# Layer 0's gated sums of rows, on four column groups instead of one

## The reference

```python
route_probs = jax.nn.softmax(xr @ wr.T, axis=-1)        # 8 routes
routes_k, indices_k = jax.lax.top_k(route_probs, 2)
gates = routes_k / jnp.sum(routes_k, axis=-1, keepdims=True)
h = jax.nn.silu(xr @ w1.T)
h = jax.nn.silu(h @ w3.T)
h = h @ w2.T
out = jnp.zeros_like(xr)
for k in range(2):
    out = out.at[indices_k[:, k]].add(gates[:, k:k + 1] * h)
```

## Time and profile before

| what | us |
|---|---|
| median of 3 runs (2851.77 to 2856.73) | 2856.41 |
| the profiled execution's own time | 2845.37 |
| its span in the profile | 2843.6 |
| TensorE busy | 2638.7 (93%) |
| VectorE busy | 1396.8 (49%) |
| ScalarE busy | 837.1 (29%) |
| layer 0 | about 0 to 1100 |
| layer 1 up to its experts | about 1100 to 1878 |

### The profile page before, as it was taken

One profiled execution on the slowest core, in us unless ns is written; L12 is line 12 of the kernel. 1 busy time (PEld: TensorE's weight loads), 2 busy tenths in 40 slices (PEclk: granted clock), 3 DMA queues, 4 the chain that ended last, 5 costly groups with the idle time before them and its releaser, 6 DMA issues. The chain is left out here.

```text
span 2843.6 us, 33688 instructions
## 1 busy us (share of the span) xinstructions
PE 2638.7 (93%) x10961; PEld 1346.8 (47%) x11021; DVE 1396.8 (49%) x2556; ACT 837.1 (29%) x1892; POOL 524.4 (18%) x563
## 2 busy tenths in 40 slices
PE   8999999999999766899999999759999999999998
PEld 4544554554455342334344334144465556655543
DVE  4546554573657263567777777507322222222255
ACT  2324332432343131145555555620011111111101
POOL 2111101110211001323233232000011111111053
PEclk9999999999999878899999999969999999999999
DMA  6120222132102103435545545240123333342155
GB/s 196 59 75 30 67 68 89 60 87 76 59 30 75 44 1 135 75 74 116 107 101 112 108 104 109 67 180 0 43 94 126 127 128 129 105 150 96 53 145 158
DMA packets 108460, 260.19 MB, mean 91 GB/s; under 512 B 19538, under 2 KB 53330, under 8 KB 96690
## 3 DMA queue, kind: packets, MB, share of 16 engines
q1 hardware_dynamic: 95634, 220.00, 26.2%
q0 software_dynamic: 11440, 37.50, 4.5%
q10 hardware_dynamic: 1264, 1.10, 0.1%
HBM read 203.27 MB, written 54.89 MB: 91 GB/s over the span
## 5 line engine op out<-in xcount | busy, mean ns | idle before, releaser
L2424 PE MATMUL d_bank<-d_w,d_xcol 128*128 x1264 | 402.5, 461 | 0.0
L1969 DVE TENSOR_REDUCE c_mx<-c_pair 128x2 f32<-128x1024 f32 x256 | 303.7, 1217 | 109.3 <-PE c_pair L1830 108.4
L1680 ACT ACTIVATE c_probs<-c_exp 128x512 f32<-128x512 f32 x512 | 277.9, 597 | 217.2 <-PE c_exp L1844 163.5
L2424 PEld LDWEIGHTS d_bank<-d_w,d_xcol 128*128 128x128 f32 x1264 | 229.0, 191 | 101.6 <-issue 2.0
L757 PE MATMUL a_bank<-a_xT,a_ring 128*128 128x512 f32 x608 | 272.5, 599 | 0.0
L508 POOL TENSOR_TENSOR a_ry<-a_rt 128x512 f32<-128x512 f32 x80 | 130.5, 1631 | 756.7 <-DVE a_rt L1009 756.7
L757 PE MATMUL a_bank<-a_wo,a_ot 128*128 128x512 f32 x512 | 222.4, 592 | 0.0
L2431 PE MATMUL d_bank<-d_w,d_hid 128*128 x480 | 219.1, 592 | 0.7 <-DVE d_hid L2662 0.7
L757 PEld LDWEIGHTS a_bank<-a_xT,a_ring 128*128 128x128 f32 x608 | 114.5, 192 | 132.3 <-issue 129.5
L2349 PE MATMUL d_bank<-d_xT,d_ws 128*128 128x512 f32 (+1 forms) x384 | 168.9, 600 | 0.7 <-ACT d_yrow L2326 0.7
L1844 PE MATMUL c_exp<-c_qs,c_ks 128*128 128x512 bf16 x453 | 146.7, 382 | 22.1 <-ACT c_probs L1680 7.9
(11 more groups left out here) (307 smaller groups left out, 3726.7 us busy)
## 6 DMA issues: line engine op xcount, KB each, us to landing
d_w<-in_w SPq DMA_DIRECT2D x16, 1408.0 KB, 6.7
scratch_results<-d_yrow SPq DMA_DIRECT2D x80, 256.0 KB
a_ring<-in_wq SPq DMA_DIRECT2D x16, 1024.0 KB, 4.8
a_wo<-in_wo SPq DMA_DIRECT2D x16, 1024.0 KB, 4.9
c_ks<-scratch_kpark SPq DMA_DIRECT2D x96, 128.0 KB, 4.7
c_qs<-scratch_qpark SPq DMA_DIRECT2D x96, 128.0 KB, 4.4
d_w<-in_w SPq DMA_DIRECT2D x16, 768.0 KB, 8.5
a_ring<-in_w SPq DMA_DIRECT2D x8, 1024.0 KB, 8.0
```

What stands on the lines that cost most here:

```text
L1680: act.activation(probs[:, (LC * CH * n + k) % RING, :], bank[:, :], ACT.Exp, scale=float(CD) ** -0.5).then_inc(exped.sem, 1)
L1969: dve.tensor_reduce(mx[:, n % 2, at0:at0 + 2], bank[:, :].rearrange("p (i n) -> p i n", i=2), AX.X, ALU.max).then_inc(maxed.sem, 1)
L2424: ins = pe.matmul(bank[:, 0:FI], xcol[:, v, k, :], w13[:, bass.ds(at, 1), which, k, :].rearrange("p a n -> p (a n)"), start=(k == 0), stop ...
```

## The change

The four matmuls of `first_rows` no longer add up in the same 8 partitions. `gate` becomes 32 columns wide for each sequence (columns 8 to 31 are zero and stay so; one GpSimd memset more, so `consts` counts ten). The matmul of sequence `b` writes the 32 partitions from `32 * b` on, each with start and stop. `fsum` becomes [128, 512] and so holds four parts, and the addition, the store, the scratch tensor and the load in layer 1 have that size. The four parts are summed where `fs` was turned: the transposes become fp32 matmuls with the constant `over` [128, 128], which has a one in rows 0 to 7, 32 to 39, 64 to 71 and 96 to 103, in the column of the route. `over` is loaded with one DMA more (64 KB). GpSimd's memset of `fs` goes, and with it SyncE's wait.

```diff
-        gate = sb("gate", [P, GB, E0])
-        fsum = sb("fsum", [E0, D])
+        gate = sb("gate", [P, GB, HD])
+        fsum = sb("fsum", [P, D])
...
-                    sp.wait_ge(consts.sem, 9)
+                    sp.wait_ge(consts.sem, 10)
...
+            pool.memset(gate[:], 0.0).then_inc(consts.sem, 1)
...
                     for b in range(GB):
-                        ins = pe.matmul(bank[0:E0, :], gate[:, b, :], h2[:, b, :], start=(b == 0), stop=(b == GB - 1))
+                        ins = pe.matmul(bank[HD * b:HD * b + HD, :], gate[:, b, :], h2[:, b, :], start=True, stop=True)
...
-                        ins = dve.tensor_tensor(gate[:, b, :], eq[:, 0, :], eq[:, 1, :], ALU.add)
+                        ins = dve.tensor_tensor(gate[:, b, 0:E0], eq[:, 0, :], eq[:, 1, :], ALU.add)
...
-                    dve.tensor_tensor(fsum[:, :], bank[0:E0, :], fsum[:, :], ALU.add).then_inc(f_added.sem, 1)
+                    dve.tensor_tensor(fsum[:, :], bank[:, :], fsum[:, :], ALU.add).then_inc(f_added.sem, 1)
...
+        over = probs[:, KC + 2, 0:P]
...
-            sp.wait_ge(consts.sem, NC)
-            sp.dma_start(probs[0:E0, KC, :], t["fsum"]).then_inc(fix_in.sem, 16)
+            sp.dma_start(fs, t["fsum"]).then_inc(fix_in.sem, 16)
+            sp.dma_start(over, t["over"]).then_inc(fix_in.sem, 16)
...
-            pool.memset(fs, 0.0).then_inc(consts.sem, 1)
...
-                        fix_in.wait(pe, 0, 3)
+                        fix_in.wait(pe, 0, 4)
                         bank = steps.start(pe, 0, ("ft",))
                         for c in range(KC):
-                            ins = pe.transpose(bank[:, c * P:(c + 1) * P], fs[:, c * P:(c + 1) * P], ident[:, :])
+                            ins = pe.matmul(bank[:, c * P:(c + 1) * P], fs[:, c * P:(c + 1) * P], over,
+                                            start=True, stop=True)
```

More of the change, by code:

```diff
@@ L537, in _ @@
             act.preload_act_table_set("natural_log_exp_and_others")
-            act.wait_ge(consts.sem, 9)
+            act.wait_ge(consts.sem, 10)
             for a, m in stages():
@@ L747, in _ @@
             pe.wait_ge(weights.sem, 16 * NW)
-            pe.wait_ge(consts.sem, 9)
+            pe.wait_ge(consts.sem, 10)
             for a, m in stages():
@@ L988, in _ @@
             dve.wait_ge(weights.sem, 16 * NW)
-            dve.wait_ge(consts.sem, 9)
+            dve.wait_ge(consts.sem, 10)
             for a, m in stages():
@@ L1375, in build_layer1 @@
         fs, ft = probs[:, KC, :], probs[:, KC + 1, :].rearrange("p (c n) -> p c n", c=KC)
+        over = probs[:, KC + 2, 0:P]
         rows = sb("rows", [E0, D])
         fstats, fmom, frstd = sb("fstats", [E0, 6]), sb("fmom", [E0, 2]), sb("frstd", [E0, 1])
-        NW, NL, NC, NS = 5, 4, 5, 2
+        NW, NL, NC, NS = 5, 4, 4, 2
         ident_in, weights, late = (signal(n, 0, 16) for n in ("ident_in", "weights", "late"))
@@ L2738, in build_program @@
     t = dict(t)
-    scratch = (("x3", [GROUPS, P, GB, D], F32), ("pre", [GROUPS, E0, D], F32), ("fsum", [E0, D], F32),
+    scratch = (("x3", [GROUPS, P, GB, D], F32), ("pre", [GROUPS, E0, D], F32), ("fsum", [P, D], F32),
                ("x5", [GROUPS, P, GB, D], F32), ("kpark", [2, P, 3, D], BF16), ("qpark", [2, P, 3, D], BF16),
@@ L2796, in constants @@
     t["ident16"] = high_halves(t["ident"])
+    t["over"] = np.zeros((P, P), f)
+    t["over"][HD * np.arange(GB)[:, None] + np.arange(E0), np.arange(E0)] = 1
     sel = np.zeros((MP, HX, P), f)
```

## The result

| | before | changed |
|---|---|---|
| median of 7 runs, us | 2856.41 (2851.77 to 2857.17) | 2845.06 (2840.74 to 2846.60) |
| ratio, with its 95% interval | | 0.9957 (0.9946 to 0.9969) |
| the profiled execution: time, span, us | 2845.37, 2843.6 | 2842.32, 2840.5 |

The change is faster by 11.3 us (difference of the medians; 0.4%), where 6.7 us were forecast; the time lies in the stated range of 2842 to 2855.5 us. Two later measurements of the same two kernels gave ratios of 0.9977 (0.9960 to 0.9995) and 0.9967 (0.9956 to 0.9979). The two profiled executions differ by 3.1 us only. So the questions are whether the steps of the forecast happened, and why executions of one kernel lie so far apart.

A forecast was written before the change was run, and what follows sets the result against it. Layer 0 was taken as bound by TensorE, busy 252.1 of 262.0 us in a stage. Terms -7.59 + 0.61 + 0.30 = -6.68 us, carried over to the median of 2856.41, gave 2849.7 us; range 2842 to 2855.5.

The forecast's parts named there:

- The product: Line 922's four matmuls, between stages of layer 0: 1.00 us to the successor instead of 3.53, saving 2.53 each.
- What follows it: Behind the product at three hand-overs between stages: everything moves 2.53 us earlier, waits keep their size, wider addition free; 7.59 saved.
- The third hand-over: Third passage between layer 0's stages, without keys, only VectorE's chain: 2.53 us saved, the 4.93 wait before the turning kept.
- The last product: Line 922's product in layer 0's last stage: saves 0, as VectorE's addition stands behind its late normalisation.
- The end store: Store of fsum at layer 0's end, 240 KB more behind the 1 MB store at 401 GB/s: +0.61 us.
- The turning: Turning of fs in layer 1, transposes replaced by fp32 products: 0.63 us becomes 0.93, so +0.30.
- The clock rival: Granted clock falls after hand-overs, 1.26 us each: two more give 2852.2 (chance 0.15), the present one vanishing 2848.4 (0.08).
- the prediction's own signs of being wrong: Layer 0's end moves by less than 5 us, or layer 1 or the experts change by more than 2.
- the forecast's own 2847 to 2852: Range for the whole program's time in us from the sum of the terms' bounds, without the slow store.
- a held stage: Rival: a transfer, such as the keys' weights, or another engine holds the next stage; two hand-overs lost, 2854.8 us, chance 0.08.

The follow-up runs named there:

- r4_vadd: Kernel before with the grouped product alone: fsum stays 8 by 512, VectorE adds the four parts one after another; 2847.18 against 2856.83 us, ratio 0.9972.
- r5_lastwide: Changed kernel with only the last stage's product undone, its four matmuls adding up over 128 columns again; ran once, 2850.14 us.
- r2_after: Changed kernel without an edit, measured again against the kernel before on the same chip; 2849.17 against 2856.83 us, ratio 0.9977.
- r1_before: Kernel before without an edit, run again for a second profile; ratio 0.9998 (0.9980 to 1.0016).
- r7_keys: Changed kernel with the fourth key tile ahead of turn_x(0) instead of behind it; 2838.57 against 2851.89 us, ratio 0.9952.

## Why the prediction was right, and where it was off

**The product, -2.53 us at a hand-over: right.** 257.4 to 254.9 in two stages, in two and three executions of the kernel before and the changed one. Layer 1's four-group products gave the price, 1.00, to the hundredth.

**What follows it: right.** The wait before the turning kept its size at both kinds of hand-over. That VectorE's wider addition costs nothing held within 0.01 us (0.69 against 0.68). r4_vadd shows how near VectorE's chain is.

**The third hand-over**: 2.49 us less from product to turning. The whole fourth stage is 128.1, 130.1 us before and 126.8, 128.2, 126.8 changed, 1.8 less in the mean; 2.5 is shown for its head only.

**The last product, 0: right**, by r5_lastwide.

**The end store, +0.61: 0.48 measured**, by the same two rows in seven profiles with the large store (8.74 to 8.76) and three with the small one and one addition (8.26 to 8.28). The price is the transfer: from its first packet to its last the two stores take 2.83 us before and 3.34 after, and from there to layer 1 it is 0.85 and 0.83. Whether the 240 KB more or their being in packets of 2 KB set the 0.51 is not shown; the forecast had the bytes at 401 GB/s.

**The turning, +0.30: 0.50 measured.** I compared lengths (0.63 with 0.93); the distances of starts are 0.56 and 1.06. The distance of starts is what a product takes from its successor, and this step did not keep to it.

**The clock rival.** It named the right mechanism and the right size (1.26 us then for the keys alone, 1.71 for a whole fall), but tied it to the hand-over. Falls come anywhere in layer 0. Their number differs by up to three in a stage, and the kernel before can be 11 us apart from itself in two profiles. That spread also trips one of the prediction's own signs of being wrong, a change of more than 2 us behind layer 0. From layer 1's start to the end the first profiles took 1743.3 and 1746.9 us, but the kernel before took 1748.1 in its second, so that sign could not tell anything.

**The size of the whole.** The steps sum to 2.53 + 2.53 + 2.49 - 0.48 - 0.50 = 6.6 us. Measured were 11.3, 7.7 and 9.5 us as differences of medians. That the first time lies in the stated range is in part luck: 2845.06 us is outside the forecast's own 2847 to 2852 (and its terms' bounds, summed, give only 2848.8 to 2851.2), and the range holds it because it was widened for the spread of executions and for a held stage. The first ratio's interval excludes 6.6 us (0.9977), the other two hold it (0.9967 up to 0.9979 only just). Beside r2_after, a part of the difference belongs to no edit. An estimate from every execution there, its span times its granted clock: the 35 of the kernel before have a mean of 2755.5 us, the changed kernel's 12 have 2746.3, 9.2 less, but r1_before's 12, the same kernel without an edit, have 2753.1, 2.4 less (0.5 is the standard error). Against those the change is worth 6.8 us. Why one kernel differs so from itself is not shown, nor whether the other measurements hold the same 2.4. What is left of the rest, chance in the sampling or a gain outside the stages that I compared, stays open: the granted clock's mean is not higher in the changed kernel, and from layer 1's start to the end the three profiles of the changed kernel took 1746.9, 1754.9 and 1743.6 us against 1743.3 and 1748.1 before, which shows no gain there and is too wide to exclude one.

## What to carry to other kernels

- Four accumulating matmuls took 3.53 us with 8 stationary columns and 3.44 with 128: few columns save nothing. Where several such matmuls add up, give each a group of 32 columns and sum the parts in a later product that is done anyway: here four took 1.00 us instead of 3.53, and the sum cost 0.50 once, the larger store 0.48.
- Before such a gain is multiplied by its count, look at each place for who comes next: at one of four places another chain ended last, VectorE's normalisation and the store behind it, and the gain was nothing.
- Where executions differ by more than the change, compare a stretch between two fixed instructions and take off what its granted clock lost; here that repeated to 0.1 us while the whole program spread by 25.

## What the runs showed of the hardware that was not expected

Single falls of the granted clock to 1.2 GHz, 1.71 us lost each, come at changing places in a TensorE-bound stretch, with TensorE busy all through the two shown. When the fourth key tile removed the wait at the hand-overs, the falls behind them went and others came: both stages of r7_keys lost 3.41 us still. A 256 KB store issued behind a 1 MB one delayed the end by 0.48 us, and a 16 KB one issued 2.7 us behind it by 0.12. Split into packets of 2 KB instead of 8 KB, the stores kept the DMA engines as full but moved 334 GB/s instead of 393.
